# Summing the four corners of a sampled tap: two pairwise adds, or one reduction along the corner axis

## What is computed

```python
value = (hh * hw * v1 + hh * lw * v2 + lh * hw * v3 + lh * lw * v4) * mask[..., None]
value = jnp.transpose(value, (0, 1, 2, 4, 3)).reshape(N, oH, oW, C * kk)
w = jnp.transpose(dcn_weight, (1, 2, 3, 0)).reshape(C * kk, -1)
return jnp.einsum('nhwc,cf->nhwf', value, w)
```

## Time and profile before

| what | value |
|---|---|
| time, median of 3 runs | 4405.45 us (4403.4 to 4419.57) |
| the profiled execution: its time, its span | 4427.31 us, 4425.5 us |
| busy share of the span | PE 66%, POOL 66%, DVE 55%, ACT 40% |
| the chain that ended last, by engine | POOL 43%, PE 23%, issue 13%, DVE 11% |

### The profile page before, as it was taken

One profiled execution on the slowest core, in us unless ns is written; L12 is line 12 of the kernel. 1 busy time (PEld: TensorE's weight loads), 2 busy tenths in 40 slices (PEclk: granted clock), 3 DMA queues, 4 the chain that ended last, 5 costly groups with the idle time before them and its releaser, 6 DMA issues.

```text
span 4425.5 us, 51603 instructions
## 1 busy us (share of the span) xinstructions
PE 2910.2 (66%) x17810; PEld 1891.5 (43%) x17810; DVE 2435.6 (55%) x3747; ACT 1761.2 (40%) x2959; POOL 2925.6 (66%) x2608
## 2 busy tenths in 40 slices
PE   5969687586757786777777676788681357146432
PEld 2434534452446345633465345633460146135321
DVE  6354454744675456655665466655654245345775
ACT  5656466245523562355425552365231112122210
POOL 0040074777777776777767777777777777776770
PEclk8979798678856895678667886589665556555555
DMA  5000214321533132423342144313351325243446
GB/s 123 8 15 9 39 24 102 100 77 50 127 96 96 39 106 82 131 54 97 85 116 77 51 110 111 110 33 107 87 133 47 104 88 131 62 127 91 121 111 120
DMA packets 540746, 375.76 MB, mean 85 GB/s; under 512 B 465872, under 2 KB 470736, under 8 KB 540496
## 3 DMA queue, kind: packets, MB, share of 16 engines
q0 software_dynamic: 110848, 257.07, 20.1%
q1 hardware_dynamic: 429648, 115.40, 12.5%
HBM read 308.79 MB, written 89.41 MB: 90 GB/s over the span
## 4 chain that ended last, share of the span: by engine, by line
POOL 43%; PE 23%; issue 13%; DVE 11%; ACT 4%; DMA 3%; DVEq 2%; SPq 1%; ACTq 0%; POOLq 0%
POOL G L548 28%; PE PS L1689 22%; POOL shared L562 9%; POOL slot_rows L554 6%; DVE G L623 2%; DMA G<-corner_table,index 2%; DVE G L629 1%; DMA out<-experts_w 1%; DVEq L625 1%; DVE small L972 1%; DVE value L631 1%; PE PS L1724 1%; DVE st L590 1%; ACT small L1551 0%; DVE smallc L590 0%
## 5 line engine op out<-in xcount | busy, mean ns | idle before, releaser
L548 POOL DMA_INDIRECT G<-corner_table,index x1800 | 2029.3, 1127 | 681.6 <-issue 537.0
L623 DVE TENSOR_TENSOR G<-G,corner_w 128x768 f32<-128x768 f32 x600 | 541.5, 953 | 678.2 <-DMA G<-corner_table,index 678.1
L1515 ACT ACTIVATE work<-PS 128x768 f32<-128x768 f32 (+2 forms) x800 | 643.2, 822 | 541.9 <-PE PS L1689 277.8
L1689 PE MATMUL PS<-xn 128*128 128x400 f16 (+3 forms) x3200 | 647.9, 346 | 236.0 <-ACT work L1515 229.8
L951 DVE TENSOR_TENSOR work<-work 128x768 f32<-128x768 f32 (+2 forms) x496 | 479.7, 973 | 457.0 <-PE PS L1689 415.3
L554 POOL DMA_INDIRECT slot_rows<-split_a,slot x400 | 485.1, 1213 | 335.1 <-DVE slot L1046 213.5
L562 POOL DMA_INDIRECT shared<-slot_results,slot x400 | 410.1, 1025 | 349.5 <-DMA slot_results<-shared 227.8
L1689 PE MATMUL PS<-work,xm 128*64 128x400 f32 (+3 forms) x3200 | 638.0, 517 | 0.0
L1689 PEld LDWEIGHTS PS<-xn 128*128 128x128 f16 (+1 forms) x3200 | 289.8, 101 | 666.4 <-ACT work L1515 389.2
L1724 PE MATMUL PS<-ident,value 128*128 128x128 f32 x800 | 181.8, 370 | 522.3 <-DVE xq L636 275.5
L1423 ACT ACTIVATE val_cm<-PS 128x512 f32<-128x512 f32 x200 | 119.1, 596 | 694.5 <-PE PS L1724 694.3
(11 more groups left out here) (266 smaller groups left out, 3591.7 us busy)
## 6 DMA issues: line engine op xcount, KB each, us to landing
G<-corner_table,index POOLq DMA_INDIRECT x1800
corner_table<-rows_scratch SPq DMA_DIRECT2D x32, 784.0 KB
shared<-slot_rows SPq DMA_DIRECT2D x32, 512.0 KB, 7.6
slot_results<-shared SPq DMA_DIRECT2D x32, 512.0 KB
corner_table<-G SPq DMA_DIRECT2D x8, 841.0 KB, 10.5
slot_rows<-split_a,slot POOLq DMA_INDIRECT x400
shared<-slot_results,slot POOLq DMA_INDIRECT x400
experts_w<-x_scratch SPq DMA_DIRECT2D x8, 784.0 KB, 6.2
```

The lines of the kernel that those rows point to most:

```text
L548: GP.indirect_dma_start(G[0:rows, n % 2, tap * 4 * C:(tap + 1) * 4 * C], None, tables[b % 2], bass.IndirectOffsetOnAxis(ap=index[0:rows, c ...
L623: V.tensor_tensor(g, g, bc(w, 2, C), ALU.mult)
L1515: A.activation(relu[0:rows, u % 2, :, 0:n], PS[u % 2][0:rows, :, 0:n], ACT.Relu).then_inc(s["relu_done"], 1)
L1689: return P.matmul(o, a, b, start=start, stop=stop, skip_group_check=True)
```

## The change

`weigh` has four pieces in place of five. Piece 3 is now a single `tensor_reduce` from `G` into `value`, which reads the gathered tile with the corner as the innermost axis: it steps over 64 numbers (256 bytes) from one read to the next, four reads for each of 576 sums, 2304 reads in all. L629 and L631 are gone. The wait on `val_tr` stands ahead of this one instruction, and `valued` is raised by it. In the mixer it stands where the first of the two adds stood (half-step 6), and nothing is left at half-step 7. The numbers summed are the same.

```diff
-MIX_SAMPLE, MIX_EVAC, MIX_ADD, MIX_WEIGH = (0, 2, 4, 6), (1, 3, 5), 7, (2, 3, 4, 6, 7)
+MIX_SAMPLE, MIX_EVAC, MIX_ADD, MIX_WEIGH = (0, 2, 4, 6), (1, 3, 5), 7, (2, 3, 4, 6)
...
                 else:
                     dve.drain()
-                    if piece == 4 and b * T + t > 0:
+                    if piece == 3 and b * T + t > 0:
                         dve.wait_ge(s["val_tr"], 2 * (b * T + t))
                     if piece == 3:
-                        V.tensor_tensor(g[:, :, 0:2, :], g[:, :, 0:2, :], g[:, :, 2:4, :], ALU.add)
-                    else:
-                        V.tensor_tensor(value[:, :].rearrange("p (n c) -> p n c", n=TAPS), g[:, :, 0, :], g[:, :, 1, :],
-                                        ALU.add).then_inc(s["valued"], 1)
+                        red(value[:, :].rearrange("p (n c) -> p n c", n=TAPS), g.rearrange("p n s c -> p n c s")).then_inc(s["valued"], 1)
...
-                for piece in range(5):
+                for piece in range(4):
```

## The result

The changed kernel takes 4432.82 us (median of 5 runs), the kernel before 4405.45 us in runs beside it: a ratio of 1.006, 95% interval 1.0033 to 1.0087. It is some 27 us slower where 31 us of gain were forecast; the time lies inside the range given. The profiled execution took 4442.78 us, span 4441.0 us.

The account below looks back on a forecast made before the run. The prediction took POOL to set the pace of the units. Its terms, -105 + 31 + 10 + 33 = -31 us, took the median of 4405 to 4374, say 4375 us, with a range of 4315 to 4480.

Parts of the forecast that it names:

- term 1: POOL in images 0 to 6: without L629's hold on an issue, 0.6 us less per tile, 175 x 0.6 = -105 us.
- d: What DVE loses on a tile by the reduction in place of the pair: 1.94 us, with bounds 0.35 and 2.52.
- term 3: Image boundary: POOL's start on tile 0 waits for tile 23's sum, 2.6 us in each of four images, +10 us.
- term 2: Routing in images 2 to 5: POOL waits longer for sums, 11d = 21 us, plus 10 us of lost savings; +31 us.
- Term 4: Expert turns: 1.80 us of ACT waits cover d, 0 us; past 1.8, each 0.1 costs 0.1 in some 54 turns.
- Term 5: Tail: rounds 7 to 22 and tile 0 pay d in full, 17 x 1.94 = +33 us.
- The hold moves: Rival, chance 0.08: POOL runs into the next add more often, 0.25 us per tile is left of term 1; 4435 us.
- DVE paces the expert turns: Rival, chance 0.25: wide reads cost about 2.2 ns, the reduction 5.4 us, DVE's product for the experts comes late; 4490 us.
- Full rate: Rival, chance 0.30: the reduction takes some 2.5 us and most of term 1 stays; 4324 us.

## Why the prediction was wrong

- **What bounds the kernel** was right in the main: the time of every run goes with POOL's work and its wait for the sums. What was not right is that a faster POOL makes all of images 0 to 6 faster, as term 1 has it: in the mixer part there was next to nothing to gain (below).
- **The reduction's length** was right, and for the reason given. What the writes with a step of 16 bytes paid, 0.69 to 0.94 ns, is about what wide reads pay: (4107 - 2553) / 2304 = 0.67 ns. The Trainium skill's 1.73 ns for an element when one of two sources hops at each ("Vector Engine (DVE) Microarchitecture Reference", section 5.2) is near the 3.62 us for 2048 reads, 1.77 ns each.
- **Term 1** (-105 us) was right in what the gathers save: 9 x 63 ns = 0.57 us a tile where 0.6 was forecast, 1800 x 63 ns = 113 us in all. The changed kernel's timeline shows why, in one tile of image 3:

```profile
2291.01 4.11 DVE L590 TENSOR_REDUCE value<-G 128x576 f32<-128x2304 f32 x1
2292.04 0.95 POOL L548 DMA_INDIRECT G<-corner_table,index  x1 [0.30 <-issue]
2293.29 0.95 POOL L548 DMA_INDIRECT G<-corner_table,index  x1 [0.30 <-issue]
2294.54 0.95 POOL L548 DMA_INDIRECT G<-corner_table,index  x1 [0.30 <-issue]
```

  The reduction does not hold POOL: over the whole trace 403 issues have nothing but it beside them, and they take 0.946 us on average, as the 358 with nothing of DVE beside them do (0.944). With the short reduction and no moved wait the ratio gives -83 us, with 19 either way, where the prediction's sum for d = 0.35 was -81.
- **The step that failed is the waits of POOL for the sum, terms 2 to 4.** They were to cost 31 + 10 + 0 = 41 us; POOL's waits in images 0 to 6 grew from 59 to 188 us, by about 130 (table above). Of the 58 us between the forecast of -31 and the 27 measured, some 32 are the moved wait (1.006 - 0.9988) and the other 26 the longer sum (with two tiles 5 us are gained, not 31; its interval is 10 us either way). This parting holds in that order only, since the moved wait costs little ahead of a short sum.
  - The **moved wait** had no price beyond d and "some 1 us" in the mixer. The prediction told where `val_tr` was moved, but took DVE's waits for PE as cover for d. A wait covers what stands ahead of it: L629 was done under it, the reduction comes behind it. Two `value` tiles take these waits away at tiles 4 and 11 to 14.
  - The **longer sum** cost more at the image boundary (tile 0: 30 us, some 6 at each of five images, where term 3 had 2.6 at each of four) and in the routing (tiles 4 to 8 with two `value` tiles: 93 against 44 us, so 49, where term 2 had 31). Of these 49, 33 stand in images 2 to 5, which term 2 counted, and 16 in images 0 and 1, which it left out and which had no wait there before. In the mixer part, tiles 17 to 24 were to bring 0.6 us each. In image 2 POOL took 138.8 us from the first gather of tile 17 (2018.6) to that of the next tile 0 (2157.4), and 141.4 after the change (2017.3 to 2158.7, of which 6.60 are the wait): all that these tiles gained was lost at tile 0, and more. It is so in images 0 to 4: 137 to 140 us before and 139 to 142 after, as POOL works 1 to 4 us less in each and waits 4.5 to 6.6 us at tile 0. Even the reduction without gaps leaves 136 to 140 us, with waits of 3.0 to 6.5 us.
  - **Term 4** (0 us) was nearly right for the length: 3 us at tiles 11 to 14 with two tiles, 20 us with the moved wait. By its own rule past 1.8 us it should have had 0.14 x 54 = 8 us at d = 1.94, and the sum -23 us.
- **Term 5** (+33 us) was somewhat high: POOL's waits in the last image grew by 22 us, and the time from its first gather to the end by 23 (462.9 to 486.3). The prediction's sign for this term was PE's wait in the tail. In the tail's round 10, before and after the change:

```profile
4137.49 1.09 PE L1724 MATMUL PS<-ident,value 128*128 128x128 f32 x4 [7.27 <-DVE xq L636]
...
4140.25 1.08 PE L1721 MATMUL PS<-ident,value 128*128 128x128 f32 x4 [9.13 <-DVE xq L633]
```

  It grew like this, by 1.8 to 1.9 us, in nine of the rounds 8 to 21. In the other five PE does not wait at this place before and waits 0.3 us at most after. So d is not paid in full in all of the rounds 7 to 22.
- **The rivals.** *The hold moves* named nearly the right time (4435 us) by a mechanism that is not there: the gathers became shorter by nearly all that term 1 had. *DVE paces the expert turns* needed a reduction past 5 us (2304 reads of 2.2 ns are 5.1 us, or 5.3 with the 0.19 us that contiguous reductions take beside their reads, rather than its 5.4). *Full rate* was wrong on the length, but its 4324 us for a short sum was close to the 0.9829 of the run without gaps. The case that came, in which POOL saves all that was forecast and gives it back as waits, was in the sum, and too small. A slower kernel had been given a chance of 0.27, most of it for that second rival.

The price of 1.93 us on the kernel before, 68 us, was forecast well. Whether a faster POOL makes each us of sum dearer is open: 0.0154 and 0.0219 do not exclude each other. Two more things were not tested: what the reduction's place in the mixer costs by itself (all of the sum now stands at half-step 6, where the second add stood at 7), and whether the moved wait would cost less if PE raised `val_tr` straight behind its transposes.

## What to carry to other kernels

When the bounding engine gets faster, list every place where it waits for another, or nearly waits, and price the slower partner at each: a saving ends at the next such place. When an instruction takes the place of two, ask which half stood ahead of a wait; work done under a wait is free, and fusing it with what follows puts all of it behind. Where an instruction's length holds another engine, cutting it into shorter ones (here 0.9816) can bring the gain without the longer chain.

## What was not expected of the hardware

The price of a step in reads is a single stage: nothing at 8 bytes, 0.63 to 0.73 ns for each number from 16 bytes on, and no more at 2048 bytes. And halving the products, which stand back to back without a gap, does free POOL between them: 1.05 and 1.10 us an issue in the tile shown, and 1091 ns on average over all gathers instead of 1116, with the first add in thirds in both.
